# Expert lists from four-token bit masks, and expert weights issued from ScalarE's queue

## The chip, the cores and the metric

The kernel runs on one core of one Trainium2 chip. The metric is the device time of one execution in microseconds (us). Its median over three runs before the change is 985.01 us (984.28 to 988.32).

## The reference, cut to what matters

The kernel computes one transformer block of the "macaron" form on 4096 tokens (8 x 512) of width 128: half a feed-forward stage, attention with 16 heads of 8, and half a feed-forward stage again with the same weights. Both feed-forward stages are a mixture of 64 experts, of which each token takes 8, plus a shared expert. An expert takes at most its first 64 tokens in token order.

```python
x = x + 0.5 * ffn(layernorm(x))
x = x + attention(layernorm(x))          # untouched by the change
x = x + 0.5 * ffn(layernorm(x))

def ffn(x):                              # x [4096, 128]
    probs = softmax(x @ router_w.T)      # 64 experts
    topk_w, topk_ids = top_k(probs, 8)
    topk_w = topk_w / sum(topk_w)
    onehot = flat_e[:, None] == arange(64)
    pos = cumsum(onehot)[..., flat_e] - 1
    valid = pos < 64                     # the first 64 tokens of each expert
    ...
    h = silu(xb @ w_gate) * (xb @ w_up)  # per expert, 64 tokens x 96
    y = h @ w_down
    routed = segment_sum(y * weight)
    shared = silu(x @ sg) * (x @ su) @ ws_down
    return routed + shared
```

## The kernel before

The 4096 tokens are NT = 32 tiles of P = 128 tokens, taken in NG = 8 groups of GT = 4 tiles. Each engine has its own program written by hand (`block.sync`, `block.gpsimd`, `block.vector`, `block.scalar`, `block.tensor`), with `ffn(ffns[0])`, `attention()` and `ffn(ffns[1])` in order, and semaphores between them. Nothing is planned by a tool: each engine works its list off in the order of the source.

The tokens come in four loads on SP's queue (L326). VectorE takes statistics (L925, L659, L661), ScalarE the square root (L937), VectorE the reciprocal (L666). Then a routing loop runs over the eight groups. GpSimd normalises (L503, L507), SP stores the normalised tokens to HBM for the later gather (L355), TensorE transposes (L1064) and makes the logits (L1069), ScalarE copies and takes the exponential (L942, L943, L946), VectorE finds the eight largest and marks them (L688 to L700). From the marks VectorE makes a key for each token and expert (L702): T minus the token's number where the expert is taken, else 0. Then it makes the routing weights (L705 to L714), which SP stores (L359). A group's normalisation waits for the store of the group two before it, as there are two buffers.

TensorE transposes the keys of all tiles into four banks of PSUM (L1082) and ScalarE copies them to SBUF (L954). There `KT` is 128 rows (64 experts for the even tiles, 64 for the odd ones) of 2048 keys. The list of an expert is its 64 largest keys, that is its first 64 tokens. `top_list` (L733) finds them eight at a time: MAX8 over the row (L735), then MATCH_REPLACE8, which takes these eight out (L737), 15 operations, each waiting for the last. It is run over the 2048 keys of each half, then over the 2 x 64 merged (L743). TensorE transposes the result (L1115), VectorE turns it into indices for gather and scatter (L746 to L752).

Beside the search runs the shared expert: TensorE (L1089, L1091, L1098), ScalarE (L959, L960, L965), GpSimd (L525, L531). It begins when the keys are copied (`wait(pe, f.kts, 4)`, L1103). When both are done, GpSimd gathers tokens for pairs of experts from HBM (L550), TensorE computes them, VectorE weights the results (L774) and GpSimd scatters them with addition into HBM (L563). SP clears these sums before with stores of zeros (L335), 640 KB each: five before the routing, four after its first group, four after its last.

The expert weights, 3 MB each for gate, up and down, are loaded once. SP issues them behind the last zeros of the first stage (L374), with one row of 96 or 128 numbers per partition and expert. TensorE waits for them ahead of the first expert (L1117).

Of the kernel before, what the change touches and what calls it, by code (L numbers as in the profile page):

```python
# [6 lines left out]
BF16 = mybir.dt.bfloat16  # L7
U32 = mybir.dt.uint32
ALU = mybir.AluOpType
ACT = mybir.ActivationFunctionType  # L10
X = mybir.AxisListType.X
P = 128


def macaron_kernel(nc, x_in, wq, bq, wk, bk, wv, bv, wo, bo, gamma, beta,
# [9 lines left out]
    T = B * S  # L25
    NT = T // P
    E, _, F = w_gate.shape
    K8, C = 8, 64
# [10 lines left out]
    NR = NPART * NPART * HD  # L39
    MR = P - 2  # L40

    SCALE = float(HD) ** -0.5
# [13 lines left out]
    with ExitStack() as ctx:  # L56
        def sb(name, shape, dt=F32):
            return ctx.enter_context(nc.sbuf_tensor(name, shape, dt))
# [50 lines left out]
        zeros = sb("zeros", [P, 10 * D])  # L109
        keyt = sb("keyt", [P, NT])  # L110
        slot_c = sb("slot_c", [P, 1])
# [25 lines left out]
        den_r = [carve(GT) for _ in range(2)]  # L137
        key = carve(NT * E)
        KT = carve(NT * E)
        cand = carve(C)  # L140
# [41 lines left out]
        def heads(stack, rows, g):  # L182
# [27 lines left out]
        s_cst1 = sem("constants_step")  # L210
        s_zero = sem("zeros_ready")
        s_rwp = sem("router_transposed")
        s_rws = sem("router_copied")
# [6 lines left out]
                      top8_found=NT, top8_marked=NT, keys_ready=NG, exp_ready=NG, masked_exp=NG, exp_sum=NG,  # L220
                      exp_recip=NG, weights_ready=NG, keys_transposed=4, keys_copied=4, list_step=38,
                      slots_transposed=1, indices_ready=1, shared_up_in_psum=NG, shared_up_copied=NG, shared_silu=NG, shared_hidden=NG,
# [17 lines left out]
        class Ffn:  # L240


            def __init__(self, p):
# [11 lines left out]
                self.ws = [n(f"weights_stored{i}") for i in range(2)]  # L255
                self.ktp, self.kts = n("keys_transposed"), n("keys_copied")
                self.rnd = n("list_step")
# [65 lines left out]
        def _(sp):  # L323
# [26 lines left out]
            def ffn(f):  # L350
# [20 lines left out]
                if f.p == 0:  # L371
                    zero_sums(0, 2, 3)
                    for w, t in ((w_gate, wg_sb), (w_up, wu_sb), (w_down, wd_sb)):
                        sp.dma_start(t[:], w.rearrange("e k n -> k e n")).then_inc(s_wexp, 16)  # L374

# [103 lines left out]
        def _(pool):  # L479
# [7 lines left out]
            f32 = dict(allow_small_or_imprecise_dtypes=True)  # L487
            pool.iota(keyt[:], pattern=[[-P, NT]], base=T, channel_multiplier=-1, **f32).then_inc(s_cst, 1)
            for half in range(2):
                rows = slice(half * C, (half + 1) * C)  # L490

                pool.wait_ge(s_cst, 3 + 2 * half)
                pool.iota(slot_c[rows, :], pattern=[[0, 1]], base=0, channel_multiplier=1, **f32).then_inc(s_cst, 1)
                pool.iota(acc_off[rows, :], pattern=[[0, NP2 // 2], [2 * ACC, 2]], base=half * ACC,
                          channel_multiplier=0, **f32).then_inc(s_cst, 1)

            def ffn(f):
                def normalise(g, r):
# [9 lines left out]
                                       ALU.mult).then_inc(f.xn.sem, 1)  # L508
                pool.wait_ge(s_cst, 7)
                wait(pool, f.rs, 1)  # L510
# [142 lines left out]
        def _(dve):  # L653
# [23 lines left out]
            def ffn(f):  # L677
# [3 lines left out]
                def route(g, r):  # L681
# [15 lines left out]
                    for j in range(GT):  # L697
# [3 lines left out]
                    wait(dve, f.rep, GT * (g + 1))  # L701
                    dve.scalar_tensor_tensor(out=kk[:, bass.ds(g * GT, GT), :], in0=d, scalar=0.5,  # L702
                                             in1=keyt[:, bass.ds(g * GT, GT)].unsqueeze(2).to_broadcast([P, GT, E]),
                                             op0=ALU.is_gt, op1=ALU.mult).then_inc(f.key.sem, 1)
                    dve.scalar_tensor_tensor(out=e_r[r], in0=d_r[r], scalar=0.5, in1=e_r[r],  # L705
# [11 lines left out]

                dve.wait_ge(s_cst, 7)
                route(0, 0)
# [213 lines left out]
        @block.scalar  # L933
        def _(act):
            def ffn(f):
                wait(act, f.ve, 1)
# [121 lines left out]
        def _(pe):  # L1058
            def ffn(f):
# [42 lines left out]
                wait(pe, f.xts, 2 * NG)  # L1102
                wait(pe, f.kts, 4)  # L1103
                up(0, 0)
# [208 lines left out]
```

## Time and profile before

| | |
|---|---|
| median of the timed runs | 985.01 us |
| profiled execution, its own time | 990.85 us |
| its span | 989.0 us |
| first routing and its lists, up to the first gather | 0 to 109 us |
| first expert stage and sums | 109 to 272 us |
| attention | 272 to 717 us |
| final normalisation of attention | 717 to 742 us |
| second routing and lists, up to the first gather | 742 to 832 us |
| second expert stage and sums | 832 to 989 us |
| TensorE busy | 681.7 us (69%) |
| VectorE busy | 682.7 us (69%) |
| ScalarE busy | 420.0 us (42%) |
| GpSimd busy | 409.3 us (41%) |

The page gives busy time as shares of the whole span; they say little here, since each stage has another limit. The chain of work that ended last, and the timeline of one stretch, show which engine the others wait for. In a timeline row the first number is the start, the second the duration, both in us; then come engine, source line, operation, what is written from what, and in brackets how long the engine had been idle and what ended that. SPq is SP's queue of DMA issues: its duration is the time in which SP is busy with the issue, not the transfer.

### The profile page before, as it was taken

The page shows a single profiled execution, that of the slowest core. Times are in us where ns is not written, and L with a number is a line of the kernel's source. Part 1 is how long each engine was busy: PE and PEld are TensorE (multiplying, and loading weights), DVE is VectorE, ACT ScalarE, POOL GpSimd, SP SyncE. Part 2 cuts the span into 40 slices and gives each one's busy share as a digit, 9 for nine tenths or more (in the row PEclk, how much of TensorE's full clock was granted, in tenths as well). Part 3 has the DMA queues.
Part 4 walks back from the last instruction along what each step waited for, and adds up shares of the span by engine and source line. Part 5 has one row for each costly group of instructions (what it writes and reads, how often), then busy time and mean ns, then how long its engine had stood idle before and what let it go on. Part 6 is the DMA issues. An engine that isn't in the chain of part 4 may idle for free.

```text
span 989.0 us, 16170 instructions
## 1 busy us (share of the span) xinstructions
PE 681.7 (69%) x4579; PEld 335.1 (34%) x4579; DVE 682.7 (69%) x1396; ACT 420.0 (42%) x885; POOL 409.3 (41%) x492
## 2 busy tenths in 40 slices
PE   2576397600389999999999999999605682886200
PEld 1443285500123333333333333332104441775100
DVE  5899332358797888888888888887276995322345
ACT  2234011000037777777777777777653350111000
POOL 2417478786622233332223333210045173788722
PEclk9998555555589999999999999999955595555555
DMA  7549733347759964444545444451102200233377
GB/s 233 202 151 292 128 51 52 47 68 207 146 74 253 240 124 91 82 88 91 96 86 93 84 85 89 93 96 34 38 0 70 59 1 23 55 51 53 32 208 216
DMA packets 247426, 103.42 MB, mean 105 GB/s; under 512 B 150713, under 2 KB 238937, under 8 KB 247385
## 3 DMA queue, kind: packets, MB, share of 16 engines
q1 hardware_dynamic: 235096, 92.44, 40.4%
q0 software_dynamic: 12288, 10.49, 7.4%
q8 instruction: 19, 0.31, 0.1%
q14 instruction: 23, 0.18, 0.1%
HBM read 58.33 MB, written 44.30 MB: 104 GB/s over the span
## 4 chain that ended last, share of the span: by engine, by line
PE 42%; DVE 22%; issue 12%; DMA 10%; POOL 6%; ACT 3%; SPq 3%; another core or an unknown queue 1%; DVEq 0%; ACTq 0%; POOLq 0%
PE psum L1223 13%; PE psum L1232 13%; PE psum L1210 10%; DMA routed_sums<-arena 5%; DVE arena L735 4%; DVE arena L737 4%; POOL arena L550 4%; DMA arena<-routed_sums 3%; DVE x_sb L789 2%; ACT arena L1022 2%; DVE arena L835 2%; PE psum L1177 2%; POOL routed_sums L563 1%; SPq L384 1%
## 5 line engine op out<-in xcount | busy, mean ns | idle before, releaser
L835 DVE TENSOR_REDUCE arena<-psum 128x2 f32<-128x1024 f32 x256 | 308.7, 1220 | 51.4 <-PE psum L1210 48.2
L1022 ACT ACTIVATE arena<-psum 128x512 f32<-128x512 f32 x512 | 282.0, 600 | 114.0 <-PE psum L1223 112.6
L1210 PE MATMUL psum<-arena 126*128 126x512 bf16 x512 | 196.8, 391 | 9.7 <-DMA arena<-qk_parts 5.0
L1223 PE MATMUL psum<-arena 128*128 128x512 bf16 x512 | 195.6, 385 | 7.3 <-ACT arena L1022 3.3
L1232 PE MATMUL psum<-arena 128*32 128x512 f32 x1024 | 136.2, 604 | 0.3
L622 POOL CAST arena<-arena 128x256 bf16<-128x256 f32 x32 | 12.7, 398 | 262.6 <-issue 260.1
L774 DVE TENSOR_SCALAR arena<-psum,arena 64x128 f32<-64x128 f32 x128 | 44.7, 350 | 110.2 <-DMA routed_sums<-arena 97.7
L563 POOL DMA_INDIRECT routed_sums<-arena x64 | 101.0, 1578 | 29.3 <-DVE arena L774 15.2
L1223 PEld LDWEIGHTS psum<-arena 128*128 128x128 bf16 x512 | 50.4, 100 | 149.2 <-ACT arena L1022 121.7
L550 POOL DMA_INDIRECT arena<-dispatch_rows,arena x64 | 62.8, 981 | 45.6 <-DVE arena L752 26.7
L789 DVE TENSOR_TENSOR x_sb<-x_sb,arena 128x512 f32<-128x512 f32 (+1 forms) x48 | 48.7, 1015 | 35.9 <-DMA arena<-routed_sums 34.0
L982 ACT ACTIVATE arena<-psum 96x256 f32<-96x256 f32 x32 | 12.2, 381 | 139.1 <-PE psum L1150 124.7
L1210 PEld LDWEIGHTS psum<-arena 126*128 126x128 bf16 x512 | 49.3, 99 | 42.5 <-DVE arena L835 14.8
L1136 PE MATMUL psum<-wd_sb,arena 96*64 96x128 f32 x256 | 35.9, 435 | 34.3 <-DVE arena L759 34.3
L1150 PE MATMUL psum<-arena,wg_sb 128*96 128x64 f32 x256 | 49.4, 374 | 7.6 <-ACT arena L979 5.9
L1069 PE MATMUL psum<-rwT,arena 128*128 128x64 f32 x128 | 31.4, 427 | 29.4 <-ACT arena L942 29.4
L1150 PEld LDWEIGHTS psum<-arena,wg_sb 128*96 128x96 f32 x256 | 43.4, 275 | 18.4 <-issue 10.7
L1150 PE MATMUL psum<-arena,wu_sb 128*96 128x64 f32 x256 | 47.6, 367 | 0.0
L1150 PEld LDWEIGHTS psum<-arena,wu_sb 128*96 128x96 f32 x256 | 44.8, 280 | 0.0
L1172 PE MATMUL psum<-ident,arena 128*128 128x128 f32 x32 | 10.9, 341 | 48.7 <-POOL arena L607 40.5
L1064 PE MATMUL psum<-ident,xn_sb 128*128 128x128 f32 x64 | 17.1, 424 | 37.7 <-POOL xn_sb L507 37.7
L735 DVE MAX8 arena<-arena 128x8 f32<-128x2048 f32 (+1 forms) x32 | 41.3, 1290 | 1.8 <-ACT arena L954 0.8
(120 smaller groups left out, 979.5 us busy)
## 6 DMA issues: line engine op xcount, KB each, us to landing
routed_sums<-zeros SPq DMA_DIRECT2D x26, 640.0 KB, 5.5
arena<-routed_sums SPq DMA_DIRECT2D x64, 256.0 KB, 4.3
arena<-qk_parts SPq DMA_DIRECT2D x128, 96.0 KB
ctx<-arena SPq DMA_DIRECT2D x32, 256.0 KB, 2.0
qk_parts<-arena SPq DMA_DIRECT2D x32, 192.0 KB, 3.7
dispatch_rows<-xn_sb SPq DMA_DIRECT2D x16, 256.0 KB, 2.3
arena<-qk_parts SPq DMA_DIRECT2D x64, 64.0 KB
arena<-ctx SPq DMA_DIRECT2D x64, 64.0 KB, 2.3
```

The source lines that it names most:

```text
L550: pool.indirect_dma_start(out=gat[k % NGB], out_offset=None, in_=xw_dram[f.p], in_offset=bass.IndirectOffsetOnAxis(ap=gidx[:, k:k + 1], ax ...
L563: pool.indirect_dma_start(out=acc_dram[f.p], in_=y_r[k % NYB], in_offset=None, out_offset=bass.IndirectOffsetOnAxis(ap=sidx[:, k:k + 1], a ...
L735: link(dve.max(dst[:, c:c + 8], src))
L737: link(dve.match_replace(src, dst[:, c:c + 8], src, 0.0))
L774: dve.tensor_scalar(y_r[k % NYB][rows, :], bank[4 + r][rows, j * D:(j + 1) * D], gat[k % NGB][rows, col:col + 1], None, ALU.mult).then_inc ...
L789: ins = dve.tensor_tensor(xs, xs, src, ALU.add)
L835: dve.tensor_reduce(mx_r[r % 2][:, 2 * p:2 * p + 2], src, X, ALU.max).then_inc(a_mx, 1)
L1022: act.activation(p_r[tau % NPB], bank[4 + tau % 2][:, :], ACT.Exp, scale=SCALE).then_inc(a_P, 1)
L1150: ins = pe.matmul(bank[2 + r][0:F, off + m * C:off + (m + 1) * C], w[:, 4 * q + m, :], gT[r][:, m * C:(m + 1) * C], start=True, stop=True)
L1210: ins = pe.matmul(bank[tau % 4][:, :], heads(q_st[r], rows, g)[:, qt * P:(qt + 1) * P], heads(k_st[r], rows, g), start=True, stop=True)
L1223: pe.matmul(bank[4 + tau % 2][:, :], keys, heads(q_st[r], rows, g), start=True, stop=True)\
L1232: ins = pe.matmul(bank[6][32 * g:32 * g + 32, :], v_r[r][:, g, kt, :], p_r[(4 * kt + g) % NPB], start=(kt == 0), stop=(kt == 3), tile_posi ...
```

## The change

It has two parts. First, the keys are no longer made per token. VectorE writes the marks as 0 or 1 in bf16. TensorE multiplies each pair of tiles with a matrix `weight_of` that holds 1, 2, 4 and 8 for the four tokens of a block, which gives a 4-bit mask for each expert and block of four tokens: 16 bf16 products of 32 columns into one bank in place of 16 fp32 transposes into four. VectorE reads them from PSUM and makes a block key (the number of blocks left, times 16, plus the mask; 0 if the mask is empty), over 512 columns. `top_list` runs over these 512 columns, and over the merged 128 as before. The 64 first blocks with a token hold the 64 first tokens, so the blocks are unpacked: the mask's bits are shifted out with integer operations, each bit gives a candidate key, and `top_list` runs once more over the 4 x 64 = 256 candidates. ScalarE's four copies of the keys and TensorE's wait for them go.

Second, the three loads of the expert weights leave SP's queue. ScalarE issues them as its first work, behind a wait for each of the four loads of tokens.

```diff
@@ buffers
+    BT = 4
+    NB = T // BT
-        keyt = sb("keyt", [P, NT])
+        weight_of = sb("weight_of", [P, P // BT], BF16)
+        block_base = sb("block_base", [P, NB // 2])
-        key = carve(NT * E)
-        KT = carve(NT * E)
+        lists = carve(2 * NT * E)
+        key = lists[:, 0:NT * E // 2].bitcast(BF16)
+        KT = lists[:, NT * E:NT * E + NB // 2]
+        candidates = lists[0:E, NT * E // 2:NT * E // 2 + BT * C]
@@ sync
-                    for w, t in ((w_gate, wg_sb), (w_up, wu_sb), (w_down, wd_sb)):
-                        sp.dma_start(t[:], w.rearrange("e k n -> k e n")).then_inc(s_wexp, 16)
@@ gpsimd, constants
-            pool.iota(keyt[:], pattern=[[-P, NT]], base=T, channel_multiplier=-1, **f32).then_inc(s_cst, 1)
+            pool.memset(weight_of[:], 0.0).then_inc(s_blk1, 1)
+            for b in range(BT):
+
+                pool.wait_ge(s_blk1, b + 1)
+                pool.affine_select(out=weight_of[:], in_=weight_of[:], compare_op=ALU.not_equal, fill=float(2 ** b), base=-b,
+                                   pattern=[[-BT, P // BT]], channel_multiplier=1).then_inc(s_blk1, 1)
...
+                pool.iota(block_base[half * E:(half + 1) * E, :], pattern=[[-2 * (P // BT) << BT, NT // 2], [-1 << BT, P // BT]],
+                          base=(NB - half * (P // BT)) << BT, channel_multiplier=0, **f32).then_inc(s_blk, 1)
@@ vector, route
-                    dve.scalar_tensor_tensor(out=kk[:, bass.ds(g * GT, GT), :], in0=d, scalar=0.5,
-                                             in1=keyt[:, bass.ds(g * GT, GT)].unsqueeze(2).to_broadcast([P, GT, E]),
-                                             op0=ALU.is_gt, op1=ALU.mult).then_inc(f.key.sem, 1)
+                    dve.tensor_scalar(kk[:, bass.ds(g * GT, GT), :], d, 0.5, None, ALU.is_gt).then_inc(f.key.sem, 1)
@@ vector, lists
-                wait(dve, f.kts, 4)
+                dve.wait_ge(s_blk, 2)
+                wait(dve, f.ktp, 1)
+                link(dve.scalar_tensor_tensor(out=KT, in0=bank[7][:], scalar=1.0, in1=block_base[:], op0=ALU.min, op1=ALU.mult))
+                link(dve.tensor_tensor(KT, KT, bank[7][:], ALU.add))
                 top_list(cand, KT)
                 link(dve.tensor_copy(merged[0:E, 0:C], cand[0:E, :]))
                 link(dve.tensor_copy(merged[0:E, C:2 * C], cand[E:2 * E, :]))
-                top_list(slots[0:E, :], merged[0:E, :])
+                top_list(block_top, merged[0:E, :])
+
+                link(dve.tensor_copy(block_bits, block_top))
+                link(dve.tensor_scalar(block_key, block_bits, BT, BT.bit_length() - 1,
+                                       ALU.logical_shift_right, ALU.logical_shift_left))
+                for b in range(BT):
+                    dve.tensor_scalar(block_bit[b], block_bits, b, 1, ALU.logical_shift_right, ALU.bitwise_and)\
+                       .then_inc(f.rnd.sem, 1)
+                step[0] += BT
+                wait(dve, f.rnd, step[0])
+                for b in range(BT):
+                    dve.scalar_tensor_tensor(out=candidates[:, b * C:(b + 1) * C], in0=block_key, scalar=float(b),
+                                             in1=block_bit[b], op0=ALU.subtract, op1=ALU.mult).then_inc(f.rnd.sem, 1)
+                step[0] += BT
+                wait(dve, f.rnd, step[0])
+                top_list(slots[0:E, :], candidates)
@@ scalar
+            for c in range(4):
+                act.wait_ge(s_x[c], 16)
+            for w, t in ((w_gate, wg_sb), (w_up, wu_sb), (w_down, wd_sb)):
+                act.dma_start(t[:], w.rearrange("e k n -> k e n")).then_inc(s_wexp, 16)
+
...
-                for b in range(4):
-                    wait(act, f.ktp, b + 1)
-                    act.activation(KT[:, b * 512:(b + 1) * 512], bank[4 + b][:], ACT.Copy).then_inc(f.kts.sem, 1)
@@ tensor
+                pe.wait_ge(s_blk1, BT + 1)
                 for u in range(NT // 2):
                     if u % 4 == 0:
                         wait(pe, f.key, (2 * u + 8) // GT)
-                    ins = pe.transpose(bank[4 + u // 4][:, (u % 4) * P:(u % 4 + 1) * P], key[:, u * P:(u + 1) * P], ident[:])
-                    if u % 4 == 3:
-                        ins.then_inc(f.ktp.sem, 1)
+                    ins = pe.matmul(bank[7][:, u * (P // BT):(u + 1) * (P // BT)], key[:, u * P:(u + 1) * P], weight_of[:],
+                                    start=True, stop=True)
+                ins.then_inc(f.ktp.sem, 1)
...
-                wait(pe, f.kts, 4)
...
-                wait(pe, f.rnd, 32)
+                wait(pe, f.rnd, 59)
```

## Rows read from the trace of the kernel before

**Rows 1.** Page, section 4: the chain that ended last, shares by line.

```profile
PE psum L1223 13%; PE psum L1232 13%; PE psum L1210 10%; DMA routed_sums<-arena 5%; DVE arena L735 4%; DVE arena L737 4%; POOL arena L550 4%; DMA arena<-routed_sums 3%; DVE x_sb L789 2%; ACT arena L1022 2%; DVE arena L835 2%; PE psum L1177 2%; POOL routed_sums L563 1%; SPq L384 1%
```

**Rows 2.** Timeline, first stage, start of the search; start us, us, engine line.

```profile
63.09 0.43 DVE L702 SCALAR_TENSOR_TENSOR arena<-arena,keyt 128x256 f32 x1 [0.19 <-DVE arena L700]
...
64.55 0.42 DVE L714 SCALAR_TENSOR_TENSOR arena<-arena 128x256 f32<-128x256 f32 x1
64.72 0.60 ACT L954 ACTIVATE arena<-psum 128x512 f32<-128x512 f32 x1 [1.49 <-PE psum L1082]
65.35 2.30 DVE L735 MAX8 arena<-arena 128x8 f32<-128x2048 f32 x1 [0.38 <-ACT arena L954]
...
70.07 2.29 DVE L735 MAX8 arena<-arena 128x8 f32<-128x2048 f32 x1
```

**Rows 3.** Timeline, first stage, end of the search up to the gather.

```profile
100.70 0.19 DVE L741 COPY arena<-arena 64x64 f32<-64x64 f32 x1
...
101.15 0.29 DVE L735 MAX8 arena<-arena 64x8 f32<-64x128 f32 x1
...
101.85 0.29 DVE L735 MAX8 arena<-arena 64x8 f32<-64x128 f32 x1
...
106.40 0.31 PE L1115 MATMUL psum<-ident,arena 64*64 64x64 f32 x1 [12.91 <-DVE arena L735]
...
108.19 0.19 DVE L752 TENSOR_TENSOR arena<-arena 128x32 uint32<-128x32 f32 x1
109.34 1.16 POOL L550 DMA_INDIRECT arena<-dispatch_rows,arena  x1 [13.44 <-DVE arena L752]
```

**Rows 4.** Timelines of GpSimd and VectorE, second stage, normalisation to gather.

```profile
742.17 1.04 POOL L503 TENSOR_TENSOR xn_sb<-x_sb,mv 128x512 f32<-128x512 f32 x1 [6.07 <-issue]
...
788.32 2.29 DVE L735 MAX8 arena<-arena 128x8 f32<-128x2048 f32 x1 [0.38 <-ACT arena L954]
...
817.64 1.26 POOL L531 TENSOR_TENSOR x_sb<-x_sb,arena 128x512 f32<-128x512 f32 x1 [0.52 <-ACT arena L965]
832.19 1.05 POOL L550 DMA_INDIRECT arena<-dispatch_rows,arena  x1 [13.29 <-DVE arena L752]
```

**Rows 5.** Timeline, first stage: shared expert's first product, last addition; first scatter.

```profile
65.46 2.00 PE L1089 MATMUL psum<-z_sb,wsgu_sb 128*96 128x512 f32 x2 [0.78 <-ACT arena L954]
...
94.64 1.26 POOL L531 TENSOR_TENSOR x_sb<-x_sb,arena 128x512 f32<-128x512 f32 x1 [0.90 <-ACT arena L965]
...
128.60 1.64 POOL L563 DMA_INDIRECT routed_sums<-arena  x1 [2.95 <-DVE arena L774]
```

**Rows 6.** Timeline of SP's queue: first zero stores, and the three weights.

```profile
14.32 3.80 SPq L335 DMA_DIRECT2D routed_sums<-zeros  x5
...
69.01 1.04 SPq L374 DMA_DIRECT2D wg_sb<-in_L_ffn_w_gate  x1
70.50 11.91 SPq L374 DMA_DIRECT2D wu_sb<-in_L_ffn_w_up  x1
82.46 9.52 SPq L374 DMA_DIRECT2D wd_sb<-in_L_ffn_w_down  x1
```

**Rows 7.** DMA issues: KB each, median us from issue to landing.

```profile
wd_sb<-in_L_ffn_w_down SPq DMA_DIRECT2D x1, 3072.0 KB, 30.6
```

**Rows 8.** Groups by line and form: busy us, mean ns, idle before.

```profile
L1223 PEld LDWEIGHTS psum<-arena 128*128 128x128 bf16 x512 | 50.4, 100 | 149.2 <-ACT arena L1022 121.7 <-issue 3.4
```

**Rows 9.** Timeline, first stage: tokens landed, square root, first and third normalisation.

```profile
10.09 1.65 DVE L925 BATCH_NORM_STATS2 stats<-x_sb 128x6 f32<-128x128 f32 x8 [0.23 <-DMA x_sb<-in_L_attn_x]
...
14.36 0.23 ACT L937 ACTIVATE rstd<-rstd 128x32 f32<-128x32 f32 x1 [12.32 <-DVE rstd L661]
...
15.13 1.04 POOL L503 TENSOR_TENSOR xn_sb<-x_sb,mv 128x512 f32<-128x512 f32 x1 [11.11 <-DVE rstd L666]
...
27.27 1.04 POOL L503 TENSOR_TENSOR xn_sb<-x_sb,mv 128x512 f32 x1 [7.85 <-DMA dispatch_rows<-xn_sb]
```

**Rows 10.** Windows: stretch, length, busy PE, PEld, DVE, ACT, POOL; PEclk, DMA share, GB/s.

```profile
20.00:30.00 10.00, 4.33 (x20) 3.75 (x20) 8.30 (x41) 2.75 (x5) 2.55 (x3) 1.00 1.03 396
...
65.44:92.00 26.56, 23.99 (x88) 11.88 (x88) 26.18 (x18) 13.88 (x24) 17.66 (x14) 1.00 1.03 326
```

More of the change, by code:

```diff
@@ L8 @@
 U32 = mybir.dt.uint32
+I32 = mybir.dt.int32
 ALU = mybir.AluOpType
@@ L137, in macaron_kernel @@
         den_r = [carve(GT) for _ in range(2)]
-        key = carve(NT * E)
-        KT = carve(NT * E)
+        lists = carve(2 * NT * E)
+        key = lists[:, 0:NT * E // 2].bitcast(BF16)
+        KT = lists[:, NT * E:NT * E + NB // 2]
+        candidates = lists[0:E, NT * E // 2:NT * E // 2 + BT * C]
+        small = lists[0:E, NT * E + NB // 2:NT * E + NB // 2 + (3 + BT) * C]
+        block_top = small[:, 0:C]
+        block_bits, block_key = [small[:, i * C:(i + 1) * C].bitcast(I32) for i in (1, 2)]
+        block_bit = [small[:, (3 + b) * C:(4 + b) * C].bitcast(I32) for b in range(BT)]
         cand = carve(C)
@@ L211, in macaron_kernel @@
         s_zero = sem("zeros_ready")
+        s_blk = sem("block_constants_ready")
+        s_blk1 = sem("block_constants_step")
         s_rwp = sem("router_transposed")
@@ L220, in macaron_kernel @@
                       top8_found=NT, top8_marked=NT, keys_ready=NG, exp_ready=NG, masked_exp=NG, exp_sum=NG,
-                      exp_recip=NG, weights_ready=NG, keys_transposed=4, keys_copied=4, list_step=38,
+                      exp_recip=NG, weights_ready=NG, keys_transposed=1, list_step=65,
                       slots_transposed=1, indices_ready=1, shared_up_in_psum=NG, shared_up_copied=NG, shared_silu=NG, shared_hidden=NG,
@@ L255, in __init__ @@
                 self.ws = [n(f"weights_stored{i}") for i in range(2)]
-                self.ktp, self.kts = n("keys_transposed"), n("keys_copied")
+                self.ktp = n("keys_transposed")
                 self.rnd = n("list_step")
@@ L487, in _ @@
             f32 = dict(allow_small_or_imprecise_dtypes=True)
-            pool.iota(keyt[:], pattern=[[-P, NT]], base=T, channel_multiplier=-1, **f32).then_inc(s_cst, 1)
+            pool.memset(weight_of[:], 0.0).then_inc(s_blk1, 1)
[3 more added lines that the diff above has]
+                                   pattern=[[-BT, P // BT]], channel_multiplier=1).then_inc(s_blk1, 1)
+            pool.wait_ge(s_blk1, BT + 1)
+            for half in range(2):
+                if half:
+                    pool.wait_ge(s_blk, half)
+                pool.iota(block_base[half * E:(half + 1) * E, :], pattern=[[-2 * (P // BT) << BT, NT // 2], [-1 << BT, P // BT]],
+                          base=(NB - half * (P // BT)) << BT, channel_multiplier=0, **f32).then_inc(s_blk, 1)
+            pool.wait_ge(s_blk, 2)
             for half in range(2):
                 rows = slice(half * C, (half + 1) * C)
-                pool.wait_ge(s_cst, 3 + 2 * half)
+                pool.wait_ge(s_cst, 2 + 2 * half)
                 pool.iota(slot_c[rows, :], pattern=[[0, 1]], base=0, channel_multiplier=1, **f32).then_inc(s_cst, 1)
@@ L508, in normalise @@
                                        ALU.mult).then_inc(f.xn.sem, 1)
-                pool.wait_ge(s_cst, 7)
+                pool.wait_ge(s_cst, 6)
                 wait(pool, f.rs, 1)
@@ L716, in route @@
                                              op0=ALU.mult, op1=ALU.mult).then_inc(f.w.sem, 1)
-                dve.wait_ge(s_cst, 7)
+                dve.wait_ge(s_cst, 6)
                 route(0, 0)
```

## The prediction

> **What bounds the kernel now.** I read the chain of work that ended last first. Its line shares [rows 1] say that most of the span is attention (L1223, L1232, L1210), which the change does not touch. But L735 and L737, the search for the expert lists on VectorE, stand in the chain with 4% each. So I went to the timeline of the two routed stages, one at each end of the kernel.
>
> In the first one, the search starts at 65.35 us [rows 2], right after the last PSUM copy of ScalarE, and the first gather starts at 109.34 [rows 3]: 44.0 us. In the second the same stretch runs from 788.32 to 832.19 [rows 4], 43.9 us. Beside it runs the shared expert, which GpSimd ends at 95.90 in the first stage [rows 5] and at 818.90 in the second [rows 4]. GpSimd then idles for 13 us until the lists are there (the idle time in the gather's row, [rows 3]). So VectorE alone sets the end of this stretch; what lies 13 us below is the shared expert. The first scatter follows 19.3 us behind the first gather, at 128.60 [rows 5], behind thirteen gathers and a wait of 2.95 us; nothing in this stretch looks at the time, so an earlier first gather moves everything behind it by as much, if the weights are there.
>
> Then the weights. SP issues them from 69.01 on; the second issue takes 11.91 us and the third 9.52 us, and nothing but the issue before stands in front of each [rows 6]. The last lands 30.6 us after its issue [rows 7], at 82.46 + 30.6 = 113.1, and TensorE starts on the experts then. That is hidden today (the first gathers land then too); it would be a wall if the lists came 14 us earlier and the weights stayed on SP.
>
> **Part 1, the search.** The masks of four tokens become one 4-bit number, so the list is searched over 512 columns, not 2048; then bits are unpacked and a third search is made over 256 columns.
> - Price of a search: one round (a maximum and a replacement) goes from one MAX8 to the next. At 2048 columns 70.07 - 65.35 = 4.72 us [rows 2], at 128 columns 101.85 - 101.15 = 0.70 [rows 3]. In between 4.02/1920 = 2.09 ns a column (1.05 for each operation). So 1.50 us at 512, 0.97 at 256.
> - Removed: 7 x 4.72 + 2.31 = 35.35 us.
> - The 512-column search: 7 x 1.50 + 0.72 = 11.25. The 128-column merge stays, 5.24 (101.15 to 106.39), and its two copies, 0.45 [rows 3].
> - Building the keys: two elementwise operations over 512 columns, from PSUM. One over 256 takes 0.42 [rows 2]; with 1.05 ns a column 0.69 each, 1.45 with gaps (bounds 1.0 and 2.0).
> - Unpacking: two dependent small operations at the 0.22 of the copies, and twice four independent ones of 64 to 256 columns at about 0.2: 2.1 us (bounds 1.5 and 3).
> - The 256-column search: 7 x 0.97 + 0.43 = 7.2.
> - Transpose and index arithmetic stay: 106.39 to 108.38, 2.0 [rows 3].
>
> Sum from start to indices: 1.45 + 11.25 + 0.45 + 5.24 + 2.1 + 7.2 + 2.0 = 29.7 us, where 43.0 stood (65.35 to 108.38).
>
> The start moves too. ScalarE's four copies go, among them the 0.60 at 64.72 [rows 2], and VectorE can start when its own last route operation ends, 64.97. The last four bf16 products must be done by then: their mask is ready at 63.52 [rows 2]; with the weight load of a bf16 tile at 0.10 [rows 8] and a few tenths for 32 columns they end near 64.2, in time. That is 0.38 us earlier. The mask itself is now a one-input operation with bf16 output; no row shows it at this size, so between the 0.43 of L702 [rows 2] and the 0.19 of a 32-column one [rows 3], eight times in a stretch that VectorE limits: 0 to 1.9 us less, I take 0.5 because 256 columns are nearer to the 0.43.
>
> What is late next is the shared expert. TensorE no longer waits for the copies, so its first product at 65.46 [rows 5] comes at about 64.2, 1.2 us earlier, and with the 0.5 GpSimd is done at 94.2; the indices are there at 64.5 + 29.7 = 94.2. A tie: a cheaper search would bring nothing more, a dearer one costs in full. First gather at 95.2, so 14.1 us earlier; in the second stage likewise. **Two stages: -28.2 us.** New constants on GpSimd (about ten small operations in the first microseconds) are covered: it idles from 4 us to 15.13, where its next row starts with 11 us of idle time [rows 9].
>
> **Part 2, the weights on ScalarE's queue.** They start at about 10.2, when the last tokens have come (VectorE's last group starts at 10.09, [rows 9]). Three issues then stand ahead of ScalarE's square root, which today runs at 14.36 [rows 9], and rstd, the normalisation, the transposes and the whole routing wait for it. What do the issues cost there? On SP the last ended at 92.0, 23 us after the first began. In the stretch from 65.44 (when the zero stores were issued) to 92.0 the DMA engines moved 326 GB/s at full share [rows 10]: 8.7 MB, of which 2.6 are the four zero stores, so 6.0 of the 9.4 MB of weights had to leave before the third issue was through. I take that as the property of a queue and not of SP: on ScalarE the same 6.0 MB, beside 3.3 MB of zero stores that SP issues from 14.32 [rows 6] and 0.3 MB of small loads. 9.6 MB at 326 to 396 GB/s (the latter in the window 20 to 30, where zeros ran [rows 10]) take 24 to 29 us; ScalarE is free at 34 to 39, I take 36. If SP stood still meanwhile, 6.0 MB would take 18.5: 28.7, the lower end. **Delay of the first routing: 21.6 us, between 14 and 25.**
>
> Given back: today the third group of tokens waits 7.85 us for stores that stand behind the zeros [rows 9]. From the first normalisation to the search the first stage takes 65.35 - 15.13 = 50.2 us, the second, with quiet queues, 788.32 - 742.17 = 46.2 [rows 4]. With the delay the zeros are gone, but the third weight still flows: 3.5 of these 4 us come back (bounds 0 and 4). The weights land by about 60 and hold nobody up. Net of part 2: +18.1 us.
>
> The Trainium skill, "DMA: Bandwidth & Descriptors", section "Issuing engines are not separate DMA queues", says that all issuing engines share the same DMA engines and that spreading saves only the issue time, usually small beside the transfer. The sharing agrees with the windows at full share; the small issue time does not agree with the 11.91 and 9.52 us rows. By the page the delay would be near nothing, which is rival B.
>
> **Sum.** -28.2 + 18.1 = -10.1 us. The profiled execution took 990.85 us (span 989.0), so 980.7 in its terms; it lies 5.8 above the median of the timed runs, and the same difference there gives 985.0 - 10.1 = 974.9. The two ends of part 2 (10 to 25 net) and 1.5 us each way for the searches put this case between 965 and 984.
>
> **Rivals.**
> - B, ScalarE is not held: the issues cost about 1 us each, as the first did (1.04, [rows 6]). For it: the weights' queue starts empty. Against: the first issue on SP took 1.04 as well, and only the next ones waited. Then the routing begins on time but its stores share the engines with 9.4 MB: 3.3 MB of zeros and 0.5 of stores at half of 340 GB/s take 22 us from 14.3, so the third group starts near 37 in place of 27.27: 0 to 10 us lost, taken as 6. -28.2 + 6 = -22: 963 us, between 957 and 970.
> - C, the gain of the lists is cut: the small operations on integers or the PSUM reads cost twice what I take, or the shared expert ends later beside the busier VectorE, some 3 us in each stage, on top of the delay. -10.1 + 6 = 981.
> - D, slower: ScalarE is held until the weights have landed, not until most have left. On SP the three took from 69.01 to 113.1, 44 us; 1 MB more on the other queue adds 3. ScalarE would be free at 57, a delay of 43 instead of 21.6: 974.9 + 21.5 = 996. It turns slower than before by 0.5% from a free ScalarE at about 51 on. Against it: SP's third issue ended 21 us before its landing.
> - E, the change doesn't do what it says: the lists come no earlier and only the delay stays. The operation count speaks against it.
>
> **Chances.** My case 0.64, B 0.20, C 0.11, D and E together 0.05. The number is that of my case, 975. The range takes in B's middle and C: 960 to 984. About 0.5%, 5 us, is what a measurement of this kernel can tell from no change. Faster by more than that: nearly all of my case, B: 0.83. Within: C and the upper tail of my case, 0.13. Slower: 0.04.
>
> **What would show it.** In the changed profile: MAX8 over 512 columns near 0.7 us, the first search 11 us long and no longer 35, and the first gather about 30.7 us after the search starts, in both stages; the tie with GpSimd's last addition. ScalarE's issues of wu and wd near 10 us each or more, the square root near 36 and not 14; the third group's wait for a store gone. The second stage, which has no weights to load, must show its 14 us alone. Wrong if the square root stays near 15 (then B), or if its delay passes 36 us (then D).

## The result, and the profile after

The changed kernel takes 992.72 us (median of 7 runs, 990.97 to 994.54), the kernel before in the same runs 984.76 us (983.41 to 988.32). The ratio is 1.0076, 95% interval 1.0059 to 1.0094: slower by 8.0 us, where 10.1 less was forecast. The measured time lies outside the range of 960 to 984 us.

The first thing to look at is ScalarE, whose timeline is here from the start of the changed kernel. ACTq is ScalarE's queue of DMA issues.

```profile
10.41 0.90 ACTq L976 DMA_DIRECT2D wg_sb<-in_L_ffn_w_gate  x1
...
11.79 13.13 ACTq L976 DMA_DIRECT2D wu_sb<-in_L_ffn_w_up  x1
24.95 17.05 ACTq L976 DMA_DIRECT2D wd_sb<-in_L_ffn_w_down  x1
42.04 1.28 ACT L980 ACT_TABLE_LOAD   x1 [30.28 <-issue]
43.34 0.23 ACT L980 ACTIVATE rstd<-rstd 128x32 f32<-128x32 f32 x1
```

The three issues stand in front of the square root, as the prediction said, but they hold ScalarE until 42.0 and not 36, and behind them comes the load of a function table, 1.28 us, that was done in the first microseconds before. The square root runs 29.0 us later than in [rows 9].

GpSimd's timeline of the first stage shows the first, third and fifth normalisation. The waits for the token stores are still there, 7.5 us and then 7.0; in the kernel before, the third group waits 7.85 [rows 9] and the fifth 3.99:

```profile
44.10 1.04 POOL L525 TENSOR_TENSOR xn_sb<-x_sb,mv 128x512 f32<-128x512 f32 x1 [37.31 <-DVE rstd L688]
...
55.87 1.04 POOL L525 TENSOR_TENSOR xn_sb<-x_sb,mv 128x512 f32 x1 [7.50 <-DMA dispatch_rows<-xn_sb]
...
67.36 1.04 POOL L525 TENSOR_TENSOR xn_sb<-x_sb,mv 128x512 f32 x1 [6.96 <-DMA dispatch_rows<-xn_sb]
```

VectorE's timeline of the new lists in the first stage, with one row for each part, one row of GpSimd's shared expert beside the copy, and GpSimd's first gather and scatter behind them:

```profile
93.81 0.68 DVE L761 SCALAR_TENSOR_TENSOR arena<-psum,block_base 128x512 f32<-128x512 f32 x1
...
95.25 0.69 DVE L755 MAX8 arena<-arena 128x8 f32<-128x512 f32 x1
...
96.77 0.69 DVE L755 MAX8 arena<-arena 128x8 f32<-128x512 f32 x1
...
106.17 1.29 POOL L547 TENSOR_TENSOR arena<-arena 96x512 f32<-96x512 f32 x1 [0.25 <-POOL x_sb L553]
106.61 0.90 DVE L764 COPY arena<-arena 64x64 f32<-64x64 f32 x1
...
112.98 0.51 DVE L768 CAST arena<-arena 64x64 int32<-64x64 f32 x1
...
113.75 1.52 DVE L772 TENSOR_SCALAR arena<-arena 64x64 int32<-64x64 int32 x4
115.30 2.70 DVE L777 SCALAR_TENSOR_TENSOR arena<-arena 64x64 f32<-64x64 int32 x4
118.03 0.42 DVE L755 MAX8 arena<-arena 64x8 f32<-64x256 f32 x1
...
119.00 0.42 DVE L755 MAX8 arena<-arena 64x8 f32<-64x256 f32 x1
...
128.21 1.15 POOL L572 DMA_INDIRECT arena<-dispatch_rows,arena  x1 [5.50 <-DVE arena L790]
...
144.77 1.64 POOL L585 DMA_INDIRECT routed_sums<-arena  x1 [0.30 <-issue]
```

A round of the search takes 96.77 - 95.25 = 1.52 us at 512 columns and 0.97 at 256, as priced. The one copy, the cast, the four shifts and the four products take 0.90, 0.51, 1.52 and 2.70 us: far above what was priced (the second copy, just behind the first, takes 0.19). The first copy starts within a product of GpSimd's and ends with it, at 107.51 and 107.46. From the first operation to the indices it is 33.4 us, where 29.7 were forecast and 43.0 stood before.

In the second stage, which loads no weights, the same stretch gives the gain alone. VectorE's first list operation and GpSimd's first gather:

```profile
801.57 0.68 DVE L761 SCALAR_TENSOR_TENSOR arena<-psum,block_base 128x512 f32<-128x512 f32 x1
...
835.10 1.05 POOL L572 DMA_INDIRECT arena<-dispatch_rows,arena  x1 [3.50 <-DVE arena L790]
```

It is 33.5 us from the start of the lists to the gather, against 43.9 in [rows 4]; the indices are there 0.8 us before the gather, 32.7 from the start. The two profiled spans are both 989.0 us, though the timed runs differ by 8.0. That needs the second profile of the kernel before, in the first experiment below.

### The profile page after: what moved, and what is told of

The parts are those of the page before. It is cut to its first block, busy times and chain, and to the rows that moved or that the text cites. A ratio compares the mean times of both kernels' runs of the same rounds, so it can differ in the third digit from the quotient of the medians.

```text
span 989.0 us, 16185 instructions
## 1 busy us (share of the span) xinstructions
PE 669.5 (68%) x4518; PEld 330.2 (33%) x4579; DVE 659.7 (67%) x1464; ACT 416.1 (42%) x879; POOL 410.0 (41%) x498
## 4 chain that ended last, share of the span: by engine, by line
PE 39%; DVE 19%; issue 13%; DMA 10%; POOL 8%; ACT 5%; ACTq 3%; SPq 2%; DVEq 0%; POOLq 0%
PE psum L1272 13%; PE psum L1263 11%; PE psum L1250 9%; DMA routed_sums<-arena 5%; POOL arena L572 5%; ACT arena L1062 4%; ACTq L976 3%; DMA arena<-routed_sums 3%; DVE x_sb L827 2%; DVE arena L755 2%; DVE arena L757 2%; DVE arena L873 2%; POOL routed_sums L585 1%; SPq L394 1%; PE psum L1226 1%
## 5 line engine op out<-in xcount | busy, mean ns | idle before, releaser
L1263 PE MATMUL psum<-arena 128*128 128x512 bf16 x451 | 172.7, 386 | 7.0 <-ACT arena L1062 3.3
L572 POOL DMA_INDIRECT arena<-dispatch_rows,arena x64 | 62.5, 977 | 27.9 <-issue 17.7
L827 DVE TENSOR_TENSOR x_sb<-x_sb,arena 128x512 f32<-128x512 f32 (+1 forms) x48 | 48.7, 1016 | 34.5 <-DMA arena<-routed_sums 32.7
L1250 PEld LDWEIGHTS psum<-arena 126*128 126x128 bf16 x512 | 49.2, 98 | 42.0 <-DVE arena L873 14.4
L1176 PE MATMUL psum<-wd_sb,arena 96*64 96x128 f32 x256 | 35.9, 434 | 34.9 <-DVE arena L797 34.8
L525 POOL TENSOR_TENSOR xn_sb<-x_sb,mv 128x512 f32 (+1 forms) x16 | 16.7, 1045 | 73.2 <-DVE rstd L688 37.3
```

Of the source, the lines that this page charges most:

```text
L572: pool.indirect_dma_start(out=gat[k % NGB], out_offset=None, in_=xw_dram[f.p], in_offset=bass.IndirectOffsetOnAxis(ap=gidx[:, k:k + 1], ax ...
L827: ins = dve.tensor_tensor(xs, xs, src, ALU.add)
L1176: ins = pe.matmul(bank[4 + r][rows, j * D:(j + 1) * D], hid[r][0:F, (2 * j + half) * C:(2 * j + half + 1) * C], wd_sb[:, e, :], start=True ...
L1250: ins = pe.matmul(bank[tau % 4][:, :], heads(q_st[r], rows, g)[:, qt * P:(qt + 1) * P], heads(k_st[r], rows, g), start=True, stop=True)
L1263: pe.matmul(bank[4 + tau % 2][:, :], keys, heads(q_st[r], rows, g), start=True, stop=True)\
```

## The experiments

Theory H: the three issues hold ScalarE, the routing starts that much later, and this is what costs more than both searches save. Theory P: the small new operations of VectorE are slow because GpSimd works beside them. The rivals stand in the expectations. Ratios are to the kernel before, timed beside each experiment, with 95% intervals.

### The kernel before, profiled once more

> The kernel before, profiled once more. The first profile has 19.3 and 19.2 us between the first gather and the first scatter, with 4.9 and 3.5 us of VectorE waiting for something that the profile doesn't name; the changed kernel and the first four experiments have 16.4 to 16.6 where the weights were there. If those waits belonged to that one execution, this one has about 16.5 in both stages and its time lies near 985. If they belong to the kernel before, it has 19 again, and 5 us of what the changed kernel gains per profile are a gain of the change.

Measured: 985.01 us in a single run, span 983.2. GpSimd's first scatter:

```profile
126.59 1.64 POOL L563 DMA_INDIRECT routed_sums<-arena  x1 [0.30 <-issue]
```

GpSimd gets to the scatter without a pause, 16.6 us behind the first gather (at 110.02), and 16.4 in the second stage. The 2.95 us wait in [rows 5] and its twin belonged to the first profiled execution, which took 5.8 us more than this one; what caused them is open. So the changed kernel's profile is compared with this one from here on: first gather 128.21 against 110.02, first gather of the second stage 835.10 against 829.49, span 989.0 against 983.2.

### The weights back on SP

```diff
             zero_sums(0, 2, 3)
+            for w, t in ((w_gate, wg_sb), (w_up, wu_sb), (w_down, wd_sb)):
+                sp.dma_start(...).then_inc(s_wexp, 16)
...
-            for c in range(4):
-                act.wait_ge(s_x[c], 16)
-            for w, t in ((w_gate, wg_sb), (w_up, wu_sb), (w_down, wd_sb)):
-                act.dma_start(...).then_inc(s_wexp, 16)
```

> The changed kernel with its second part undone: the three weight loads go back to SP's queue behind the last zero stores. Theory H (ScalarE is held by the issues, and this is what made the change slow): the square root runs at 14.4 us again and the search starts near 64.5. The lists are there about 33 us later, near 98, but the weights still land near 113, so the first expert stage starts no earlier than before; only the second stage gains, 11 us. Near 973 us. Rival L (the lists themselves are slow, the hold is made good elsewhere): no faster than before, 985 or more.

Measured: 970.59 us, 0.9858 (0.9827 to 0.9889). The lists alone are a gain of 15.4 us, and the changed kernel, which adds the second part, takes 22.1 us more. GpSimd's first gather, TensorE's first transpose and GpSimd's first scatter:

```profile
98.25 1.15 POOL L574 DMA_INDIRECT arena<-dispatch_rows,arena  x1 [4.78 <-DVE arena L792]
...
111.86 0.69 PE L1162 MATMUL psum<-ident,arena 128*128 128x128 f32 x2 [16.23 <-DMA wd_sb<-in_L_ffn_w_down]
...
122.10 1.64 POOL L587 DMA_INDIRECT routed_sums<-arena  x1 [7.57 <-DVE arena L814]
```

The wall that the prediction named is there: TensorE waits for the third weight until 111.9, and the first scatter comes 23.9 us behind the gather instead of 16.5. It takes only part of the first stage's gain, since TensorE has a slack of some microseconds before it delays the scatter.

### The weights on ScalarE's queue alone, with the lists as before

```diff
         def _(act):
+            for c in range(4):
+                act.wait_ge(s_x[c], 16)
+            for w, t in ((w_gate, wg_sb), (w_up, wu_sb), (w_down, wd_sb)):
+                act.dma_start(...).then_inc(s_wexp, 16)
```

> The kernel before with only the second part: the three weight loads on ScalarE's queue, lists as they were. Theory H: the square root moves from 14.4 to about 43 us and the first gather by about 28 to 29 us, with nothing given back; the second stage is unchanged. Near 1013 us. By the recorded prediction's giving back of 3.5 us and a hold of 21.6 it would be 1003. Rival L: less than 5 us slower than before.

Measured: 1013.99 us, 1.0285 (1.0268 to 1.0303), 28.0 us slower. ScalarE's timeline and the first gather:

```profile
42.47 0.23 ACT L940 ACTIVATE rstd<-rstd 128x32 f32<-128x32 f32 x1
...
137.44 1.16 POOL L548 DMA_INDIRECT arena<-dispatch_rows,arena  x1 [13.39 <-DVE arena L750]
```

The square root is 28.1 us later than in the kernel before, the gather 27.4 us later than in its second profile, and the whole 28.0 us slower. The hold costs in full: at most 0.7 us of it comes back in the first routing, no more than the two profiles of the kernel before differ there (109.34 and 110.02). With the new lists the same hold gives 992.7, so the lists save 21.3 us and the hold costs 28.0.

### Only two weights on ScalarE's queue

```diff
-            for w, t in ((w_gate, wg_sb), (w_up, wu_sb), (w_down, wd_sb)):
+            for w, t in ((w_gate, wg_sb), (w_up, wu_sb)):
                 act.dma_start(...)
...
             zero_sums(0, 2, 3)
+            sp.dma_start(wd_sb[:], ...).then_inc(s_wexp, 16)
```

> The changed kernel with two weights on ScalarE's queue, the third on SP behind the last zero stores. Theory H, with the rule that an issue ends when most of the load before it has left: the second issue ends near 25 us as in the changed kernel, there is no third, and the square root runs near 26, 17 us earlier than in the changed kernel. The whole is 15 to 19 us faster than the changed kernel: 974 to 978. If the issues end only with the queue's content landed, the square root is no earlier than 35.

Measured: 978.49 us, 0.992 (0.9903 to 0.9937), 14.2 us faster than the changed kernel and just outside the 15 to 19 expected. ScalarE's timeline, and GpSimd's third normalisation:

```profile
11.82 12.45 ACTq L977 DMA_DIRECT2D wu_sb<-in_L_ffn_w_up  x1
24.30 1.28 ACT L981 ACT_TABLE_LOAD   x1 [12.51 <-issue]
25.60 0.23 ACT L981 ACTIVATE rstd<-rstd 128x32 f32<-128x32 f32 x1
...
40.71 1.04 POOL L526 TENSOR_TENSOR xn_sb<-x_sb,mv 128x512 f32 x1 [10.06 <-DMA dispatch_rows<-xn_sb]
```

The square root is 17.7 us earlier, at the place the theory gave. The gain is 3.5 us less: the third group now waits 10.06 us for its store, in place of 7.50. The second weight, issued at 11.82 and 33.4 us on its way, lands at 45.2, so it is still under way. That it and the zero stores make the wait longer, and that the rest of the hold had hidden a part of this traffic, is read from this order in time and not tested alone.

### The weights in 24 pieces, spread over SP's queue

```diff
+    def weights(n):
+        for _ in range(n):
+            w, t, e = pieces.pop(0)
+            sp.dma_start(t[:, e:e + 8, :], w[e:e + 8].rearrange("e k n -> k e n")).then_inc(s_wexp, 16)
+    for g in range(2, NG):
+        store(g, g % 2)
+        store_w(g - 1, (g - 1) % 2)
+        weights(2)
     store_w(NG - 1, 1)
+    weights(len(pieces))
     zero_sums(0, 2, 3)
...
```

ScalarE's three loads go, as in the first of these experiments.

> The changed kernel with the weights on SP in 24 pieces of 8 experts: two pieces behind the stores of each of the groups 2 to 7, the rest behind the routing and ahead of the last zero stores. Theory H: no piece is large enough to hold the queue, the square root is at 14.4, the weights land before 95 us and the first gather comes near 98. Both stages gain 11 us: about 963. If stores of the routing are delayed by the pieces, up to 5 us more. By the rival that transfers beside the routing cost as much as the hold: no better than the kernel with the weights back on SP.

Measured: 963.82 us, 0.9776 (0.976 to 0.9793). GpSimd's first gather and scatter:

```profile
98.62 1.15 POOL L585 DMA_INDIRECT arena<-dispatch_rows,arena  x1 [5.45 <-DVE arena L803]
...
115.21 1.64 POOL L598 DMA_INDIRECT routed_sums<-arena  x1 [0.30 <-issue]
```

Here both walls are gone, the hold of ScalarE and the late weights, and both stages show their gain: 22.1 us, from lists that save about 11 us in each. The rival falls: the weights' transfers beside the routing cost nothing that these numbers can tell. From the first normalisation to the lists it is 49.2 us, near the 48.9 with the weights on SP at the end.

### GpSimd's work beside the lists cut to a few columns

```diff
-  pool.tensor_tensor(shh[r][0:F, :], shs[r][0:F, :], shu[r][0:F, :], ALU.mult)
+  pool.tensor_tensor(shh[r][0:F, 0:8], shs[r][0:F, 0:8], shu[r][0:F, 0:8], ALU.mult)
...
-  pool.tensor_tensor(xs, xs, shy..., ALU.add)
+  pool.tensor_tensor(xs[:, :, 0:2], xs[:, :, 0:2], shy...[:, :, 0:2], ALU.add)
```

> The kernel with the weights in pieces on SP, with GpSimd's product and sum of the shared expert cut to 8 of 512 columns and 2 of 128 (so most of the shared expert's output is left out). Theory P (the small operations of the new lists on VectorE are slow because GpSimd works beside them on wide tiles): the copy falls from 0.9 to 0.2 us, the cast from 0.5 to 0.2, the four shifts from 1.5 to 0.8, the four products from 2.7 to 0.8; about 3.6 us less in the first stage and 2.8 in the second, near 957.5 us. Rival I (integer operands are slow by themselves): shifts and products stay at 1.5 and 2.7, the time at 963.

Measured: 957.0 us, 0.972 (0.9703 to 0.9736), 6.8 us less than the kernel that it is made from. VectorE's timeline:

```profile
77.22 0.18 DVE L781 COPY arena<-arena 64x64 f32<-64x64 f32 x1
...
82.88 0.18 DVE L785 CAST arena<-arena 64x64 int32<-64x64 f32 x1
...
83.32 0.49 DVE L789 TENSOR_SCALAR arena<-arena 64x64 int32<-64x64 int32 x4
83.85 0.62 DVE L794 SCALAR_TENSOR_TENSOR arena<-arena 64x64 f32<-64x64 int32 x4
```

Copy, cast, shifts and products fall from 0.90, 0.51, 1.52 and 2.70 to 0.18, 0.18, 0.49 and 0.62 us; the first gather comes 4.0 us earlier. Theory P holds, and rival I falls: the shifts and products still read integers. ScalarE's 0.58 us operations and TensorE's products of the shared expert run beside the list operations in both kernels, so it is GpSimd's width that counts. The Trainium skill, "SBUF — State Buffer", section "Who interferes with whom", says that copies, casts and tensor_scalar can take a pair of ports that VectorE shares with GpSimd, that operations with two SBUF inputs use its read side, and that one-input operations outside the two-port modes don't contend. The rows agree: the search's maxima, with one input, took 0.69 and 0.42 us beside GpSimd's wide tiles and take the same beside the narrow ones.

### The first zero stores moved behind the routing

```diff
-            zero_sums(0, 0, 3)
...
                 if f.p == 0:
+                    zero_sums(0, 0, 3)
                     zero_sums(0, 2, 3)
```

> The changed kernel with SP's first five zero stores moved behind the routing, so that ScalarE's weights have the DMA engines almost alone while they are issued. Theory H with the byte rule (6.0 MB must leave before the third issue is through, at 326 GB/s: 18.5 us): ScalarE is free near 29 to 30 and not 42, the square root near 31, the whole 11 to 13 us faster than the changed kernel: near 980. If the length of the hold is a property of the issues and not of the traffic beside them, the square root stays near 43.

Measured: 985.68 us, 1.0011 (1.0 to 1.0022), 7.0 us faster than the changed kernel. ScalarE's timeline:

```profile
24.65 9.99 ACTq L976 DMA_DIRECT2D wd_sb<-in_L_ffn_w_down  x1
...
35.96 0.23 ACT L980 ACTIVATE rstd<-rstd 128x32 f32<-128x32 f32 x1
```

The window of its hold, columns as in [rows 10]:

```profile
10.27:34.65 24.38, 0.34 (x1) 0.18 (x1) 4.04 (x42) 0.63 (x1) 0.00 (x0) 1.00 0.91 263
```

The same window of the changed kernel:

```profile
10.40:42.00 31.60, 0.34 (x1) 0.18 (x1) 4.05 (x42) 0.42 (x1) 0.00 (x0) 1.00 0.95 312
```

The hold gets shorter by 7.3 us, 7.1 of them in the third issue, so its length does depend on the traffic beside it. But it ends at 34.65 and not at 29 to 30. The bytes are right: 24.38 us at 263 GB/s are 6.4 MB, small loads included, where the rule had 6.0 of weights; in the changed kernel 31.6 us at 312 GB/s are 9.9 MB, where I had 9.6. The rate is not. This kernel's hold, cut into stretches, shows where:

```profile
10.27:18.00 7.73, 0.34 (x1) 0.18 (x1) 4.04 (x42) 0.63 (x1) 0.00 (x0) 1.00 0.77 199
18.00:22.00 4.00, 0.00 (x0) 0.00 (x0) 0.00 (x0) 0.00 (x0) 0.00 (x0) 1.00 1.06 309
22.00:26.00 4.00, 0.00 (x0) 0.00 (x0) 0.00 (x0) 0.00 (x0) 0.00 (x0) 1.00 0.70 210
26.00:34.65 8.65, 0.00 (x0) 0.00 (x0) 0.00 (x0) 0.00 (x0) 0.00 (x0) 1.00 1.08 324
```

The start of the changed kernel's hold, and its last two microseconds:

```profile
10.40:18.00 7.60, 0.34 (x1) 0.18 (x1) 4.05 (x42) 0.42 (x1) 0.00 (x0) 1.00 0.77 203
...
40.00:41.00 1.00, 0.00 (x0) 0.00 (x0) 0.00 (x0) 0.00 (x0) 0.00 (x0) 1.00 0.69 214
41.00:42.00 1.00, 0.00 (x0) 0.00 (x0) 0.00 (x0) 0.00 (x0) 0.00 (x0) 1.00 0.36 111
```

Weights by themselves do run at 324 GB/s once they run, as on SP (326 in [rows 10]). What the forecast lacked is the first 7.7 us, at 199 GB/s, and a dip where an issue ends: the second one here ends at 24.65. The changed kernel has the same start and a dip before 42.0. Why the loads start slowly, and what makes the dip, is open.

### The pieces on ScalarE's queue

```diff
             for w, t in ((w_gate, wg_sb), (w_up, wu_sb), (w_down, wd_sb)):
-                act.dma_start(t[:], ...)
+                for e in range(0, E, 8):
+                    act.dma_start(t[:, e:e + 8, :], w[e:e + 8]...)
```

> The changed kernel with the three loads cut into 24 of 8 experts, all still on ScalarE's queue at the same place. If a queue takes a certain amount of outstanding work, whatever the size of a load, the last issue ends near 40 to 43 us as before and the time stays near 992. If only a large load holds its engine, 24 issues of about 0.6 us end near 25 and the time is near 976.

Measured: 998.67 us, 1.0146 (1.0125 to 1.0166), 5.9 us slower than the changed kernel. ScalarE's timeline, and behind it the window of its hold:

```profile
10.11 19.60 ACTq L977 DMA_DIRECT2D wg_sb<-in_L_ffn_w_gate  x8
29.73 9.65 ACTq L977 DMA_DIRECT2D wu_sb<-in_L_ffn_w_up  x8
39.42 10.88 ACTq L977 DMA_DIRECT2D wd_sb<-in_L_ffn_w_down  x8
```

```profile
10.10:50.30 40.20, 0.34 (x1) 0.18 (x1) 4.11 (x42) 0.00 (x0) 0.00 (x0) 1.00 1.06 295
```

Both readings that I had written down fall: the hold ends neither near 25 nor near 42, but at 50.3. That is 8.3 us later than in the changed kernel, and the whole is 5.9 us slower: some 2.3 us come back in the routing, where the third group waits 0.80 us for its store in place of 7.50 and the fifth 11.44 in place of 6.96. By then 40.2 us at 295 GB/s, 11.9 MB, have moved; without 3.3 of zeros and about 0.3 of small loads that is 8.3 of 9.4 MB. Three pieces were left, where whole loads leave 3.1 MB, one load. So the queue does not take a fixed amount of bytes. With pieces it took fewer bytes ahead, and cutting the loads without spreading them made the hold longer. The window's rate, 295 GB/s, is also lower than the 312 with whole loads. What the limit counts is not settled by one size.

### The zero stores behind everything

```diff
-            zero_sums(0, 0, 3)
...
-                    zero_sums(0, 1, 3)
+                    weights(2)
...
                     weights(len(pieces))
-                    zero_sums(0, 2, 3)
+                    zero_sums(0)
...
-                pool.wait_ge(s_acc0[f.p], ...)       # ahead of the first gather
+                    if k == 0:                       # ahead of the first scatter
+                        pool.wait_ge(s_acc0[f.p], ...)
```

> The kernel with the weights in pieces on SP, with all 13 zero stores of the first stage behind the last piece, and GpSimd's wait for them ahead of the first scatter and not of the first gather. In the first stage 50 to 51 us lie between the first normalisation and the search in every kernel so far, whatever is moved, and 45 to 46 in the second. Theory Z (the token stores that stand behind zero stores in SP's queue make the difference): with no zeros ahead of them the first stage takes 46 to 47 too, the first gather comes at about 94.5 in place of 98.6, the time is near 960. Rival: the pieces that now stand there hold the stores as much, and the time stays at 964 or is worse, as the zeros then land beside the gathers.

Measured: 960.96 us, 0.9758 (0.9739 to 0.9776), 2.9 us less than with the pieces alone. GpSimd's third and fifth normalisation, and VectorE's first list operation:

```profile
20.04 1.04 POOL L536 TENSOR_TENSOR xn_sb<-x_sb,mv 128x512 f32 x1 [0.59 <-DMA dispatch_rows<-xn_sb]
...
32.62 1.04 POOL L536 TENSOR_TENSOR xn_sb<-x_sb,mv 128x512 f32 x1 [7.95 <-DMA dispatch_rows<-xn_sb]
...
61.10 0.68 DVE L773 SCALAR_TENSOR_TENSOR arena<-psum,block_base 128x512 f32<-128x512 f32 x1
```

Without zeros ahead the third group waits 0.59 us in place of 7.71, but the fifth, with weight pieces ahead of its store, 7.95 in place of 4.08. Together they wait 3.3 us less, and that is the gain: from the first normalisation (15.18) to the lists it is 45.9 us, against 49.2 with zeros ahead and 46.0 in the second stage. Theory Z holds. The edit also moved GpSimd's wait for the zeros, which lies behind this stretch and adds nothing to it. This is the fastest kernel of the study that computes everything, 24 us below the kernel before.

## Why the prediction was wrong

Much of the mechanism was right: the gain of the lists, the hold of ScalarE, the wall of the late weights, the 11-us first search. Three steps failed, all towards the slow side, and they add up: the length of the hold, the store waits that were to be given back, and the small operations of the lists.

| term | forecast | measured | miss |
|---|---|---|---|
| square root later by | 21.6 | 29.0 | +7.4 |
| given back in the first routing | 3.5 | 0 | +3.5 |
| lists, first stage | 29.7 | 33.4 | +3.7 |
| lists, second stage | 29.7 | 32.7 | +3.0 |
| sum of the misses | | | +17.6 |
| whole kernel | -10.1 | +8.0 | +18.1 |

- **The hold.** The step was "9.6 MB at 326 to 396 GB/s take 24 to 29 us; ScalarE is free at 34 to 39". The bytes were right to 0.3 MB, the rate was not: both ends of it came from stretches in which the queues were full and the DMA engines' share was 1.03. The hold's window has share 0.95 and 312 GB/s, below the lower end, because it takes in the start. The forecast of 36 means 9.6 MB in 25.8 us, 372 GB/s. At that rate the 1.5 MB of the first 7.6 us would have taken 4.1 us, so by this estimate the start alone is 3.5 of the 6.0 us that ScalarE was free too late, and the last two microseconds are another 1.1. The last 1.3 us of the 7.4 are the table load, which I had not moved along with the issues. That is the term with the largest miss, and the range for it, 14 to 25, ended below what came.
- **Given back.** I wrote that "with the delay the zeros are gone" and took 3.5 of 4 us. Here the mechanism failed too: the waits for the stores are 7.50 and 6.96 us after, and from the first normalisation to the lists it is 49.7 us, against 48.9 with the weights back on SP. The third weight landed at 24.95 + 34.8 = 59.8, and four more zero stores went out at 55.3, so the stores still had company. The experiment with the weights alone on ScalarE shows the sum: square root 28.1 us later, kernel 28.0 us slower. I had in hand that the two stages differ by 4 us, and was right that store waits make that difference (the last experiment), but not that the hold would remove them. Only where the hold outlasted nearly all of the weights, with the pieces on ScalarE, did some 2.3 us come back.
- **The lists.** The searches, the block keys, the merge and the transpose came as priced, within 0.2 us each. The miss is in the two copies (1.15 us for 0.45) and the unpacking (5.05 for 2.1). I priced them from rows in which GpSimd was idle: the copies of [rows 3] run at 100.7 us, after its last addition at 94.64 [rows 5]. In the shorter lists they fall beside the shared expert. The rows to see it by were in the trace of before: an elementwise operation of 0.42 us takes 1.29 where it starts with one of GpSimd's.

```profile
37.13 1.04 POOL L507 TENSOR_TENSOR xn_sb<-xn_sb,rstd 128x512 f32<-128x512 f32 x1 [0.17 <-POOL xn_sb L503]
37.16 1.29 DVE L705 SCALAR_TENSOR_TENSOR arena<-arena 128x256 f32<-128x256 f32 x1
```

- **What held.** The bf16 products were in time, the lists started right behind VectorE's last routing operation, and the mask operation took 0.29 us instead of 0.42 in most groups. With the weights on SP a part of the first stage's gain was lost to a wall (first scatter at 122.10 against 115.21). The 0.4 us that the start was to gain over the ScalarE copy is not shown: in the second profile of the kernel before, no idle time stands ahead of the search. The tie with the shared expert did not come about: it ends at 122.7, the lists at 127.3.
- **The rivals.** B (no hold) is refuted by the rows of ScalarE's queue. The slower rival D wanted ScalarE held until the weights had landed, at about 57; it was free at 42.0 with the last weight landing at 59.8, so D's mechanism is refuted too, while its sign came. The deciding point was set as a free ScalarE at 51 for a loss of 5 us; with nothing given back the lists save 29.0 - 8.0 = 21.0 us, so break-even is a delay of 21.0, just what I had forecast for it (21.6). Rival C, at 0.11, had the size of the lists' miss right (3 us in each stage, 3.7 and 3.0 came) and not its cause: neither the integers nor the PSUM reads (0.68 and 0.69 us, as priced) were slow. I had put all doubt about the lists and all doubt about the hold in different cases, though both could be late together.

## What to carry to other kernels

A DMA issue has a length, and it belongs to the engine that issues: here three issues and a table load put a square root off by 29 us. Price it from the nearest issue that waited, with the DMA rate of the window in which it will stand and not that of a full queue, and look at what is queued behind. Spreading the large loads in pieces between the stores of SP, which computes nothing, was better than giving them to ScalarE at the start: the same lists gave 963.8 us with the one and 992.7 with the other. Cutting them without spreading them was no help. And price a small VectorE operation by who works beside it at its new time, not at its old one.

## What the runs showed of the hardware

- A queue was held, and still served its neighbour: within ScalarE's 13.13 us issue SP issued five zero stores in 4.88 us (17.21 to 22.09), against 3.80 in [rows 6] and 4.37 in the second profile of the kernel before. Four small loads that SP issued from 11.01 us on took it 3.26 us in place of 1.88. The Trainium skill, "Perfetto Trace Analysis", section "DMA Instruction — HWDGE (DVE, Sync)", says that the descriptor generator is locked for exclusive use while an issue generates. No run here separates generating from waiting, but SP was only slowed, and not shut out for the length of ScalarE's issue.
- In the changed kernel an issue ended before the load ahead of it had landed, by 5.9 and 2.6 us: the second one at 24.9 us, with the first landing at 10.4 + 20.4 = 30.8; the third at 42.0, with the second landing at 11.8 + 32.8 = 44.6.
- The weights' loads began slowly and then ran at the rate of a full queue: 199 GB/s over the first 7.7 us, 324 GB/s in the last 8.7 us of the hold, with no zero stores beside them.
- Twenty-four issues of 384 KB held ScalarE 8 us longer than three of 3 MB, for the same bytes.
- Four products of 64 x 64 took 2.70 us beside GpSimd's wide tiles and 0.62 us beside narrow ones. MAX8 and MATCH_REPLACE8 over 512 columns did not change (0.69 and 0.68 us in both).
